# A graph layer with a LayerNorm in front: the weight matrix applied after the sum over adj, LayerNorm taken off TensorE, and four equal groups of output blocks

## The reference

```python
h = jnp.maximum(_layernorm(x, axis=-1), 0.0)     # (x - mean) / sqrt(var + 1e-5), by row
support = jnp.matmul(h, W)
out = jnp.matmul(adj, support) + b
x = x + jax.nn.relu(out)
```

## Time and profile before

| | us |
|---|---|
| time, median of 3 runs | 763.18 (762.74 to 763.41) |
| the profiled execution: span, first to last instruction | 760.3 |
| the profiled execution: what lies around the span is not in its page; the median less the span | 2.9 |
| TensorE busy with matmuls | 747.8 (98%) |
| VectorE busy | 644.2 (85%) |
| ScalarE busy | 536.4 (71%) |
| GpSimd busy | 16.9 (2%) |
| DMA, mean rate | 364 GB/s |

### The profile page before, as it was taken

The page is one execution under the profiler, slowest core; times in us unless marked ns, Lnnn a source line. Parts: engine busy times, 40 slices in busy tenths (PEclk is TensorE's granted clock), DMA queues, the critical chain, the costliest instruction groups (busy, mean ns, idle before and its releaser), DMA issues.

```text
span 760.3 us, 10345 instructions
## 1 busy us (share of the span) xinstructions
PE 747.8 (98%) x3360; PEld 615.6 (81%) x3360; DVE 644.2 (85%) x452; ACT 536.4 (71%) x421; POOL 16.9 (2%) x24
## 2 busy tenths in 40 slices
PE   6999999999999999999999999999999999999997
PEld 4888888888888888788888888888788888888886
DVE  2988888888888888898889888888999898888987
ACT  3766666666666666787777777777877777777775
POOL 0000000000000000000000000000000000000000
PEclk9999999999999999999999999999999999999999
DMA  8899898999999989989999999999999999999997
GB/s 344 350 342 356 331 363 331 335 358 338 349 352 333 357 320 337 357 336 382 391 372 380 395 385 390 375 379 404 386 362 390 394 383 383 392 387 393 367 394 300
DMA packets 32987, 277.04 MB, mean 364 GB/s; under 512 B 3664, under 2 KB 3792, under 8 KB 8528
## 3 DMA queue, kind: packets, MB, share of 16 engines
q1 hardware_dynamic: 32976, 276.90, 94.4%
HBM read 272.70 MB, written 4.19 MB: 364 GB/s over the span
## 4 chain that ended last, share of the span: by engine, by line
PE 97%; ACT 1%; DVE 1%; issue 1%; DMA 0%; ACTq 0%
PE banks L425 61%; PE banks L432 30%; PE banks L381 2%; PE banks L367 2%; PE banks L378 2%; DVE xT L311 0%; DMA xT<-x_blocks 0%; ACT adj_high L269 0%; ACT relu_out L241 0%; DVE rectified L292 0%; ACT squares L234 0%; PE banks L404 0%; DVE var_eps L297 0%; ACTq L261 0%; ACTq L240 0%
## 5 line engine op out<-in xcount | busy, mean ns | idle before, releaser
L339 DVE TENSOR_TENSOR adj_low<-adj_tile,adj_high 128x2560 fp32r<-128x2560 f32 (+1 forms) x191 | 573.7, 3004 | 99.9 <-ACT adj_high L269 99.0
L269 ACT ACTIVATE adj_high<-adj_tile 128x2560 fp32r<-128x2560 f32 (+1 forms) x191 | 476.0, 2492 | 197.2 <-issue 89.7
L425 PE MATMUL banks<-adj_high,sup_high 128*128 128x512 f32 x1019 | 272.9, 398 | 1.3 <-ACT relu_out L241 1.3
L425 PE MATMUL banks<-adj_high,sup_low 128*128 128x512 f32 x1019 | 264.8, 390 | 0.0
L432 PE MATMUL banks<-adj_low,sup_high 128*128 128x512 f32 x1019 | 262.2, 389 | 0.0
L425 PEld LDWEIGHTS banks<-adj_high,sup_high 128*128 128x128 f32 x1019 | 190.9, 188 | 47.7 <-issue 6.7
L425 PEld LDWEIGHTS banks<-adj_high,sup_low 128*128 128x128 f32 x1019 | 191.8, 188 | 39.6
L432 PEld LDWEIGHTS banks<-adj_low,sup_high 128*128 128x128 f32 x1019 | 191.4, 188 | 39.7
L253 ACT ACTIVATE sup_high<-support 128x128 fp32r (+1 forms) x192 | 56.1, 292 | 0.0
L321 DVE TENSOR_TENSOR sup_low<-support,sup_high 128x128 fp32r<-128x128 f32 x192 | 54.6, 285 | 0.9 <-ACT sup_high L253 0.9
L378 PEld LDWEIGHTS banks<-mean_col,squares 128*128 128x128 f32 x128 | 18.2, 208 | 7.2 <-ACT squares L234 3.1
(11 more groups left out here) (18 smaller groups left out, 19.3 us busy)
## 6 DMA issues: line engine op xcount, KB each, us to landing
adj_tile<-adj SPq DMA_DIRECT2D x127, 1280.0 KB, 7.6
adj_tile<-adj SPq DMA_DIRECT2D x64, 1536.0 KB, 8.4
xT<-x_blocks SPq DMA_DIRECT2D x16, 256.0 KB, 8.3
out_blocks<-xT SPq DMA_DIRECT2D x1, 2560.0 KB, 13.4
out_blocks<-xT SPq DMA_DIRECT2D x6, 256.0 KB, 2.5
adj_tile<-adj SPq DMA_DIRECT2D x5, 256.0 KB, 5.7
W_sb<-W SPq DMA_DIRECT2D x1, 64.0 KB, 2.1
bias<-b SPq DMA_DIRECT2D x1, 0.5 KB, 3.1
```

Source lines behind the costliest of these rows:

```text
L269: nc.scalar.activation(adj_high[:, r % SPLIT_SLOTS, 0:width], adj_tile[:, r, 0:width], ACT.Copy).then_inc(high_ready, 1)
L339: nc.vector.tensor_tensor(adj_low[:, r % SPLIT_SLOTS, 0:width], adj_tile[:, r, 0:width], adj_high[:, r % SPLIT_SLOTS, 0:width].bitcast(F32 ...
L425: last = nc.tensor.matmul(banks[:, n % PSUM_BANKS, :], sup[:, r, :], adj[:, r % SPLIT_SLOTS, c * BANK:(c + 1) * BANK], start=opens and i = ...
```

## The change

1. W moves behind the sum: adj @ (h @ W) becomes (adj @ h) @ W. The finished sum of a block is itself split by ScalarE and VectorE (`sum_high`, `sum_low`) and multiplied by the halves of W into the same bank, three matmuls of 512 columns; then relu with bias, and the residual is added.
2. LayerNorm works on x in its own row layout, rows on partitions: row sums and means on VectorE, squares with their sum on ScalarE (four instructions of 128 columns for four tiles), power and (x - mean) * rstd on GpSimd (one power and four instructions of 128 columns), relu into `h_high` on ScalarE, `h_low` on VectorE. Both halves are kept for all 64 tiles, so the later groups split only adj.
3. Four groups of 4 blocks. Groups 0 and 2 use banks 0 to 3, groups 1 and 3 banks 4 to 7. A step is 12 products and one load of 128 x 2048. The blocks of a finished group are drained, projected and stored one by one, every fourth step of the next group.
4. x is no longer kept: four slots take x in rows during the first group, then x in blocks as the residual. There are three slots for high halves. The loops are written out. The first tile comes in pieces of 1, 1 and 2 blocks.

```diff
-WIDTHS = [6, 5, 5]
-FIRST_BLOCK = [0, 6, 11]
-SPLIT_SLOTS = 2
+WIDTHS = [4, 4, 4, 4]
+FIRST_BLOCK = [0, 4, 8, 12]
+FIRST_BANK = [0, 4, 0, 4]
+RAW_SLOTS, HIGH_SLOTS, LOW_SLOTS = 4, 3, 2
+OPENING = [1, 1, 2]
+BATCHES = [(0, 1), (1, 4)] + [(t, t + 4) for t in range(4, TILES, 4)]
+X_SLOTS = 4
+DRAIN_AT, DRAIN_EVERY = 3, 4
+PROJECT_AFTER, RELU_AFTER, STORE_AFTER = 1, 5, 10
+OUT_SLOTS = 2
...
@@ GpSimd @@
+            for j, (first, end) in enumerate(BATCHES):
+                pool.wait_ge(var_ready, j + 1)
+                nc.gpsimd.tensor_tensor(rstd[:, first:end], var_eps[:, first:end],
+                                        minus_half[:, first:end], ALU.pow).then_inc(rstd_ready, 1)
+                pool.wait_ge(rstd_ready, j + 1)
+                if j >= 3:
+                    pool.wait_ge(h_low_ready, BATCHES[j - Z_SLOTS][1])
+                for t in range(first, end):
+                    cols = slice(t % 4 * P, t % 4 * P + P)
+                    nc.gpsimd.tensor_scalar(z_sb[:, x_slot(j) % Z_SLOTS, cols],
+                                            x_sb[:, x_slot(j), cols],
+                                            neg_mean[:, t:t + 1], rstd[:, t:t + 1],
+                                            ALU.add, ALU.mult).then_inc(z_ready, 1)
...
@@ ScalarE, after the split of step t @@
+                j = (t - 1) // 4 + 2
+                if g == 0 and j < len(BATCHES):
+                    first = BATCHES[j][0]
+                    if t % 4 == 1:
+                        square(j, range(first, first + 2))
+                    if t % 4 == 2:
+                        square(j, range(first + 2, first + 4))
+                    if t % 4 == 0:
+                        rectify(j)
+                n = drained_at(t, 0)
+                if n is not None:
+                    act.wait_ge(products_done, FIRST_STEP[group_of(t)])
+                    sum_to_high(n)
+                n = drained_at(t, RELU_AFTER)
+                if n is not None:
+                    relu(n)
...
@@ VectorE @@
+            def rectified_low(j):
+                first, end = BATCHES[j]
+                at = first % 4
+                dve.wait_ge(h_high_ready, j + 1)
+                nc.vector.scalar_tensor_tensor(h_low[:, first:end, :],
+                                               z_sb[:, x_slot(j) % Z_SLOTS, at * P:(at + end - first) * P]
+                                               .rearrange("p (t d) -> p t d", d=P),
+                                               0.0, h_high[:, first:end, :].bitcast(F32),
+                                               ALU.max, ALU.subtract).then_inc(h_low_ready, end - first)
...
+                if g == 0 and j < len(BATCHES):
+                    if t % 4 == 2:
+                        variance(j)
+                    if t % 4 == 0:
+                        rectified_low(j)
+                        if j + 1 < len(BATCHES):
+                            mean(j + 1)
...
@@ TensorE @@
-                    if stage_a and r == 2:
-                        center(k + 2)
...
-                if stage_a:
-                    project(k + 2)
...
+            def project(n):
+                slot = n % OUT_SLOTS
+                out = banks[:, bank_of(n), :]
+                if n == 0:
+                    pe.wait_ge(W_low_ready, 1)
+                pe.wait_ge(sum_low_ready, n + 1)
+                nc.tensor.matmul(out, W_high[:, :], sum_high[:, slot, :], start=True, stop=False)
+                nc.tensor.matmul(out, W_low[:, :], sum_high[:, slot, :], start=False, stop=False)
+                nc.tensor.matmul(out, W_high[:, :], sum_low[:, slot, :], start=False, stop=True) \
+                  .then_inc(projected, 1)
...
+                if opens and g >= 2:
+                    pe.wait_ge(relu_ready, FIRST_BLOCK[g - 1])
...
+                n = drained_at(t, PROJECT_AFTER)
+                if n is not None:
+                    project(n)
```

More of the change, by code:

```diff
@@ new lines, in add_x @@
+            def add_x(n):
+                dve.wait_ge(relu_ready, n + 1)
+                dve.wait_ge(res_landed[n % X_SLOTS], 16 * (n // X_SLOTS + 1))
+                nc.vector.tensor_tensor(x_sb[:, n % X_SLOTS, :], x_sb[:, n % X_SLOTS, :],
+                                        relu_out[:, n % OUT_SLOTS, :], ALU.add).then_inc(output_ready, 1)
+            mean(0)
+            variance(0)
+            rectified_low(0)
+            opening(0)
+            mean(1)
+            opening(1)
+            variance(1)
@@ new lines, in _ @@
+            h_is_there(0, h_high_ready, False)
+            for i in range(len(OPENING)):
+                pe.wait_ge(opening_high, i + 1)
+                if i == 0:
+                    pe.wait_ge(h_low_ready, 1)
+                for c in range(sum(OPENING[:i]), sum(OPENING[:i + 1])):
+                    product(0, c, 0, h_high, high, 0, start=True)
+                    last = product(0, c, 0, h_low, high, 0)
+            last.then_inc(high_used, 1)
+            for i in range(len(OPENING)):
+                if i < len(OPENING) - 1:
+                    pe.wait_ge(opening_low, i + 1)
+                else:
+                    pe.wait_ge(low_ready, 1)
+                for c in range(sum(OPENING[:i]), sum(OPENING[:i + 1])):
+                    last = product(0, c, 0, h_high, low, 0)
@@ new lines, in _ @@
+            last.then_inc(products_done, 1)
+            for t in range(1, LAST):
+                g = group_of(t)
+                s = t - FIRST_STEP[g]
+                order = [(c, k) for k in range(DEPTHS[g]) for c in range(WIDTHS[g])]
+                opens, closes = s == 0, s == STEPS[g] - 1
+                pe.wait_ge(high_ready, t)
+                h_is_there(t, h_high_ready, False)
+                if opens and g >= 2:
+                    pe.wait_ge(relu_ready, FIRST_BLOCK[g - 1])
+                for c, k in order:
+                    product(t, c, k, h_high, high, t % HIGH_SLOTS, start=opens and k == 0)
+                h_is_there(t, h_low_ready, True)
+                for c, k in order:
+                    last = product(t, c, k, h_low, high, t % HIGH_SLOTS)
+                last.then_inc(high_used, 1)
+                pe.wait_ge(low_ready, t + 1)
+                for c, k in order:
+                    last = product(t, c, k, h_high, low, t % LOW_SLOTS, stop=closes and k == DEPTHS[g] - 1)
+                last.then_inc(products_done, 1)
+                n = drained_at(t, PROJECT_AFTER)
+                if n is not None:
+                    project(n)
@@ new lines, in _ @@
+            t = LAST
+            g = group_of(t)
+            for c in range(WIDTHS[g]):
+                pe.wait_ge(closing_high, c + 1)
+                for k in range(DEPTHS[g]):
+                    product(t, c, k, h_high, high, t % HIGH_SLOTS)
+                    product(t, c, k, h_low, high, t % HIGH_SLOTS)
+                pe.wait_ge(closing_low, c + 1)
+                for k in range(DEPTHS[g]):
+                    last = product(t, c, k, h_high, low, t % LOW_SLOTS, stop=k == DEPTHS[g] - 1)
+                last.then_inc(closing_products, 1)
@@ L448 @@
+            for c in range(WIDTHS[g]):
+                project(FIRST_BLOCK[g] + c)
 def kernel(x, adj, L0_gnn_W, L0_gnn_b):
```

577 lines of the change are left out of this document (280 added, 297 removed).

## The result

| | before | after |
|---|---|---|
| time, us (runs of one chip, side by side) | 763.26 (762.74 to 763.41) | 797.98 (794.99 to 800.63) |
| ratio, 95% interval | | 1.046 (1.043 to 1.049) |
| span of the profiled execution | 760.3 | 797.9 |
| its time less its span | | 1.8 |

A forecast was written before the change was run, and what follows sets the result against it. TensorE, busy 747.8 of 760.3 us, was taken as the bound. Head 11.6 + products 696.3 + projections 8.2 + tail 8.8 = span 724.9, 727.8 as a time; with 2 for DMA, 730 us, range 724 to 777.

The forecast's parts named there:

- The price of the products: TensorE over adj: 0.2267 us per 512-column product, 2.72 us for a step of 12, 696.3 us in all.
- The projections: Multiplication of finished sums by W on TensorE: 0.68 us a block, 12 of 16 in the body, 8.2 us.
- The tail: After the last product over adj: last projections, relu, residual add and store take 8.8 us, against 4.6 before.
- the changes of group: Between groups of blocks: TensorE's stalls, 2.5 us in all, go because the next group uses the other four banks.
- The splits on both engines: Splitting an adj step into high and low halves: 1.93 us on ScalarE, 2.29 us on VectorE.
- The rate of the DMA: Loads: 385.5 GB/s asked per step, 409.6 with x in the first group, which is at the limit, not over.
- The head: Start of the kernel: first product near 6.3 us instead of 17.95; head worth 11.6 us against 19.1.
- The GpSimd step: First group's LayerNorm on GpSimd: a shift 0.3 us, variance to last shift 2.3; up to 5.1 free before TensorE waits.
- rival A: First group: GpSimd shifts and two-input VectorE operations exclude each other, 1.7 to 3.6 us a batch, 754 to 782; chance 0.36.
- The DMA step: Loads by rate: first group at the limit, later groups 530.9 against 530.4 us if 395 GB/s; 2 us taken.
- Rival B: DMA becomes the bound at 387 GB/s: first group +10 us, the others +12, time 737 to 752; chance 0.12.
- loads of 10.5 and 9.95: First group, per four steps of 10.88 us: VectorE works 10.5 us, ScalarE 9.95; both fit.

The follow-up runs named there:

- run 3: The changed kernel with eight slots for adj in place of four: 773.26 us, ratio 1.014.
- 5: The changed kernel with five slots for adj in place of four: 773.45 us, ratio 1.014.
- 6: The changed kernel with the LayerNorm shifts on VectorE instead of GpSimd and eight slots for adj: 750.12 us, ratio 0.983.
- run 7: The changed kernel with eight adj slots and first-group low halves reading zeroed PSUM banks, the high half's subtraction left out there: 735.52 us, ratio 0.964.
- run 8: The changed kernel with eight adj slots and LayerNorm up to the shifts four steps earlier, relu unmoved, nothing left out: 737.49 us, ratio 0.967.
- run 9: Eight slots and LayerNorm a batch earlier, plus relu and h's low half one step before the batch's end, row sums apart: 733.70 us, ratio 0.961.
- run 12: The changed kernel with LayerNorm a batch earlier, its side work spread over the steps, and five adj slots: 736.75 us, ratio 0.965.
- run 1: The changed kernel, four slots, with first-group low halves reading zeroed PSUM banks, the high half's subtraction left out there: 766.10 and 779.54 us.
- run 10: The changed kernel, four slots, with each GpSimd shift replaced by a constant fill that reads nothing, LayerNorm's values left out: 768.94 us.
- run 2: The changed kernel, four slots, with the LayerNorm shifts on VectorE instead of GpSimd: 758.08 to 773.92 us in five runs, ratio 0.999.

## Why the prediction was wrong

**Right.** The price of the products, 2.720 us a step (3, 5 to 9, 12). The projections: with eight slots the 16 steps with projections cost 2.867 - 2.720 = 0.147 more each and the next 16 0.035, together 2.9 us a group; forecast 4 x 0.68 = 2.7. The tail: 8.3 for 8.8. No wait at the changes of group. The splits on both engines. The rate of the DMA: 393 GB/s over 140 us with five slots, 416 in the first group of 7.

**The head: 1.6 us too short.** The low half of step 1 starts at 15.47, not 13.9, and the first product at 6.97, not 6.3. The squares were right: they start 0.40 us apart (8.12, 8.52, 8.91). ScalarE was idle for 2.9 us until the first two pieces of adj had landed (it could start the first at 5.67, and the first relu stands behind it), and for 2.47 until the shifts of the second batch were done, the first of which met a low half of VectorE; ScalarE's row, then GpSimd's:

```profile
12.91 0.52 ACT L256 ACTIVATE h_high<-z_sb 128x384 fp32r<-128x384 f32 x1 [2.47 <-POOL z_sb L235]
```

```profile
10.64 1.38 POOL L235 TENSOR_SCALAR z_sb<-x_sb,neg_mean,rstd 128x128 f32<-128x128 f32 x1
```

The prediction does not list its steps between 6.3 and 13.8, so which share of the 1.6 is whose stays open.

**The GpSimd step failed, by +43 us.** It reads: "I take 0.3", and "Even at 1.01 the chain of 5.1 just fits". Alone the shift is 0.45, between the bounds; but the chain got the wait through two low halves as well. What happened is rival A's mechanism, at its price: 2.87 us per round, within 1.7 to 3.6, and over the 2.4 from which it decides the sign. In detail it is simpler than the rival's story: a shift waits for a whole run of back-to-back VectorE operations, and VectorE is hardly held in this kernel (mean 2292 ns against 2.29 forecast; 2.46 where a shift came first, run 8). What misled me was the overlap in the earlier trace rows, which I counted against the rival. There the power starts inside `sup_low`, whose last 0.12 us it overlaps. A held power ends 0.87 us after the operation that held it (run 12); by that, an estimate, one behind `sup_low` ends 0.12 + 0.87 = 0.99 us after its own start, within its usual 1.01. So a wait was there to be had, but too short to show. The split at 25.09 met only the last quarter of a microsecond of a power, and what happens in a power's first part it could not tell. In the batch above the power starts before the low half (104.19, 104.31) and is not held; in run 12 it starts after, and is, for 2 us. So 4 columns are no protection either: what counted was who came first and how much of the other was left, not how much is read. That the wait is one for SBUF reads is shown from both sides: runs 1 and 7 take away VectorE's second SBUF input, run 10 GpSimd's reads, and either is enough.

The Trainium skill ("SBUF — State Buffer", section Who interferes with whom) says just this: a VectorE instruction with two SBUF inputs against a GpSimd instruction that reads SBUF, not one that only writes, and the loser blocks. These runs agree: 1247 ns, 466 and 206. The prediction held two overlaps of 0.12 and 0.25 us against it.

**The DMA step failed, by +27 us.** It reads: "So the first group is at the limit but not over it", and for the later groups it weighs 530.9 against 530.4. It compares rates only. What binds is the circle of a slot: load 7.0 to 8.1, split 1.93, low half 2.30, against 4 x 2.72 = 10.88. The trace of before had the same circle, 13.6 us for 12.8, but not its new size: with the landing time of 7.6 us cut by a fifth as the bytes are, 6.1, the new turn is 10.3 us and fits into 10.88; with 7.6 as it stood it is 11.8 and does not. It would have shown a risk that no term of the sum held. Rival B had the place right (ScalarE waiting for adj, share 0.98 at 372 GB/s) and its size, with 387 GB/s, at +12 of the 27; but its mechanism, DMA at its top rate, is refuted by runs 3 and 5, where the same queue moves more.

**What each was worth.** Alone, the slots give 24.7 us (3) and the shifts' wait about 32 (1, at 766.10); together 62.5 (7), 6 more than the sum, because without the wait the first group meets the circle of the slots as well: 187.2 us with four slots, 179.4 with eight. Without either one the time is back inside the range of 724 to 777 (773 and 766), though not below the 763 of before; it took both to put it at 798. With both gone, run 7's span of 733.6 is 8.7 over the forecast 724.9: 1.2 in the head, 5.3 in the first group, the rest behind it. That group goes at 2.82 us a step in its middle, 11.29 us for four. Neither engine is full there: from 100 to 180 us VectorE is busy for 73.8 of 80 and ScalarE for 67.5. But they wait for each other, ScalarE 7.4 us for the shifts and 5.1 for the row means, VectorE 6.1 for ScalarE. The prediction's loads of 10.5 and 9.95 in 10.88 us fit; it put these waits at nothing. Run 9's spread order aims at them, but its profile does not settle how much they cost. The time is only 5.5 over, since 1.8 us lie around the span for my 2.9, and the 2 for the DMA were not needed.

**Open.** Why a load takes 7 us and more with four slots, but 6.0 with five, at a higher rate. The bursts above suggest it: slots released together are filled by loads issued together, and the last of them queues behind the others. That was read, not tried. Kernels with four slots also scatter, 766.1 and 779.5 for the same one (run 1), 758 to 774 (run 2), where eight slots gave 772.81 to 773.48 (run 3), though 733.35 to 738.23 in run 9; why, is open too.

## What to carry to other kernels

When a change makes the step shorter, compute the circle of each buffer (load from issue to landing, plus every consumer until release) against slots times the new step; a DMA rate that fits says nothing of it, and one more slot may be all that is missing. Before an operation is moved to GpSimd, look at what VectorE is doing at the moment when it reads SBUF: beside back-to-back operations with two SBUF inputs it waited through two and three of them, so give it a batch of lead, or one of the inputs a place in PSUM. And a short overlap in the trace is evidence against a wait only if the wait would have been long enough to see: compare it with what an operation that was held takes after its release.

## What the runs showed of the hardware that I had not expected

- A GpSimd operation of 0.45 us took 3.74 us through two VectorE operations in a row, in run 9 up to 6.40; it does not get in between two that follow each other directly. Even the power of 4 columns took 3.15 us instead of 1.01.
- Fills on GpSimd beside the same splits: 206 ns, 203 to 209, no wait at all.
- The DMA engines' busy share of 0.98 at 372 GB/s did not mean a full queue: the same loads went on to 393 at 1.00 with five slots, and to 416 at 1.01 in the first group of run 7.
- The landing time of a 1 MB load grew with the slots from 4.9 us (three) to 7.0 (four), while the rate rose only from 342 to 372 GB/s; with five it fell to 6.0 at 393, and with eight it was 8.3 at 389 (all rates from 560 to 700 us).
- VectorE is held as well where GpSimd's shift starts first: 13 low halves of run 8 took 2.45 to 2.47 us instead of 2.29.
